# Post-norm decoder layer on one core: bias scaling to ScalarE, context passes to POOL, first key packings shared between two queues, two v transposes moved

## The reference, cut to what matters

```python
x = layernorm(x + attention(x))          # 32 heads of 32, qkv = x @ qkvw + qkvb, softmax, then @ ow + ob
q1 = fake_quant(x, x1_scale, x1_zp)      # (clip(round(x/s + z), 0, 255) - z) * s
q2 = fake_quant(ctx, x2_scale, x2_zp)    # ctx: 2 batches of 1024 x 1024
x = layernorm(x + matmul(q1, q2))
x = layernorm(x + lora_moe_ffn(x))       # base matmul, 8 experts of rank 16, top 2
```

## Time and profile before

| | |
|---|---|
| median of 3 runs | 778.38 us (775.95 to 780.17) |
| the profiled execution | 779.7 us, its span 777.9 us |
| mean granted TensorE clock | 0.970 |
| TensorE busy | 733.4 us, 94% of the span |
| VectorE, ScalarE, POOL busy | 482.5, 428.4 and 200.7 us |
| steps 0 and 1 / steps 2 to 17 / what follows | 5 to 52 us / to about 500 us / to 778 us |

### The profile page before, as it was taken

The page is one execution under the profiler, slowest core; times in us unless marked ns, Lnnn a source line. Parts: engine busy times, 40 slices in busy tenths (PEclk is TensorE's granted clock), DMA queues, the critical chain, the costliest instruction groups (busy, mean ns, idle before and its releaser), DMA issues.

```text
span 777.9 us, 11948 instructions
## 1 busy us (share of the span) xinstructions
PE 733.4 (94%) x3567; PEld 538.4 (69%) x3576; DVE 482.5 (62%) x853; ACT 428.4 (55%) x924; POOL 200.7 (26%) x149
## 2 busy tenths in 40 slices
PE   7889999999999999999999997889999977999996
PEld 5668668668767767767766842367767756788884
DVE  6767566557556656656755753456676778566554
ACT  5348668668668668667767785443434471212111
POOL 6260140240230230330330000033533374122111
PEclk9989999999999999999999986799999999999999
DMA  8735436436445445444442664274454121122101
GB/s 296 232 93 186 111 84 193 110 87 191 111 98 177 111 110 163 115 131 138 115 116 76 217 185 135 80 234 161 140 185 142 74 83 55 59 78 93 70 28 54
DMA packets 55553, 99.45 MB, mean 128 GB/s; under 512 B 11104, under 2 KB 22112, under 8 KB 54624
## 3 DMA queue, kind: packets, MB, share of 16 engines
q1 hardware_dynamic: 54944, 98.26, 41.4%
q10 hardware_dynamic: 576, 0.79, 0.4%
HBM read 56.54 MB, written 16.91 MB: 94 GB/s over the span
## 4 chain that ended last, share of the span: by engine, by line
PE 61%; issue 16%; DVE 10%; POOL 5%; DMA 3%; SPq 2%; ACT 2%; ACTq 1%; DVEq 0%; POOLq 0%
PE bank L459 35%; PE bank L522 8%; PE bank L548 8%; PE bank L562 6%; POOL xb L1093 2%; DVE st L1307 2%; POOL mv L1043 1%; DMA ctx_scratch<-ctxs 1%; PE bank L478 1%; ACTq L828 1%; DMA xres<-in_x 1%; DVE x1s L1405 1%; PE bank L675 1%; POOL xres L1038 1%; DVE big_lo L1342 1%
## 5 line engine op out<-in xcount | busy, mean ns | idle before, releaser
L801 ACT ACTIVATE probs<-bank 128x512 f32<-128x512 f32 x256 | 154.8, 606 | 128.8 <-PE bank L548 126.2
L1231 DVE TENSOR_REDUCE m_col<-bank 128x1 f32<-128x512 f32 x256 | 172.3, 687 | 80.1 <-PE bank L522 79.5
L806 ACT ACTIVATE bank<-bank,m_col 128x512 f32<-128x512 f32 x256 | 171.4, 670 | 19.1 <-DVE m_col L1231 13.4
L459 PE MATMUL bank<-big_hi,w_hi 128*128 128x512 f32 x384 | 157.7, 411 | 5.4 <-DVE big_lo L1123 5.4
L459 PE MATMUL bank<-big_lo,w_hi 128*128 128x512 f32 x384 | 153.5, 400 | 0.0
L459 PE MATMUL bank<-big_hi,w_lo 128*128 128x512 f32 x384 | 151.9, 396 | 0.0
L522 PE MATMUL bank<-kp,qp 96*128 96x512 f32 x256 | 106.5, 416 | 4.4 <-ACT bank L806 4.4
L548 PE MATMUL bank<-qp,kp 98*128 98x512 f32 x256 | 109.7, 430 | 0.0
L459 PEld LDWEIGHTS bank<-big_hi,w_hi 128*128 128x128 f32 x384 | 73.8, 192 | 24.3 <-DVE big_lo L1123 5.9
L1028 POOL TENSOR_SCALAR c_raw<-c_raw,sc 128x1024 f32<-128x1024 f32 x16 | 19.3, 1203 | 270.7 <-DMA c_raw<-in_ctx 265.1
L459 PEld LDWEIGHTS bank<-big_hi,w_lo 128*128 128x128 f32 x384 | 73.4, 191 | 17.2
(11 more groups left out here) (137 smaller groups left out, 1045.6 us busy)
## 6 DMA issues: line engine op xcount, KB each, us to landing
w_raw<-in_wqkv SPq DMA_DIRECT2D x7, 1536.0 KB, 8.8
c_raw<-in_ctx SPq DMA_DIRECT2D x16, 512.0 KB, 4.0
qp<-q_hi SPq DMA_DIRECT2D x128, 64.0 KB, 2.0
kp<-k_hi SPq DMA_DIRECT2D x120, 64.0 KB, 2.0
big_raw<-in_xT SPq DMA_DIRECT2D x16, 256.0 KB, 5.7
qp<-q_lo SPq DMA_DIRECT2D x64, 64.0 KB, 2.0
c_scratch<-c_q SPq DMA_DIRECT2D x16, 256.0 KB, 2.2
r_all<-r_scratch SPq DMA_DIRECT2D x64, 64.0 KB, 2.0
```

The source lines that it names most:

```text
L459: mm = nc.tensor.matmul(dst, lhs[a], rhs[b], start=(k == 0 and n == 0) if first is None else False, stop=(k == last_k and n == 2))
L801: nc.scalar.activation(probs[:, j, t, :], bank(ST0 + i % 2), ACT.Exp).then_inc(sem["exp_ok"], 1)
L806: nc.scalar.activation(bank(MAX[n % 3]), bank(MAX[n % 3]), ACT.Exp, bias=m_col[:, n:n + 1], accum_out=l_col[:, 1 - par, n:n + 1]).then_inc ...
L1231: nc.vector.reduce_max(m_col[:, n:n + 1], bank(MAX[n % 3]), AX, negate=True).then_inc(sem["rowmax"], 1)
```

## The change

ScalarE scales the q bias, before it rounds the v weights; DVE no longer does. POOL does all three passes over a context tile, one behind the other. For the keys of unit 0 ScalarE issues only heads 0 and 1; SyncE issues those of heads 2 and 3 between its q packings, and its load of the next weights in step 0 stands behind all packings. The v transpose of step 1 stands at slot 8 (was 16), that of step 2 at slot 8 (was at the start), both into PROJ0, and DVE's copies of both stand after maximum n = 2.

```diff
@@ SyncE, step
                     if begin:
                         pack(s, par, 1, "q")
-                    else:
-                        wait_alone(sp, sem["lo_ok"], 2 * s + 2)
+                    wait_alone(sp, sem["lo_ok"], 2 * s + 2)
+                    if not begin:
                         pack(s, par, 0, "k")
                         pack(s, par, 1, "k")
-                    if begin:
-                        load_w()
                     if 2 not in early:
                         pack(s, par, 2, "q")
...
                 if proj:
-                    if not begin:
-                        pack(s, par, 2, "k")
+                    pack(s, par, 2, "k")
                     if 3 not in early:
                         pack(s, par, 3, "q")
-                    if not begin:
-                        pack(s, par, 3, "k")
+                    pack(s, par, 3, "k")
+                    if begin:
+                        load_w()
@@ TensorE
-                        mm = nc.tensor.transpose(bank(ST0 + 1 if second else PROJ0, t * P, (t + 1) * P), vT[:, t * P:(t + 1) * P], ident[:, :])
+                        mm = nc.tensor.transpose(bank(PROJ0, t * P, (t + 1) * P), vT[:, t * P:(t + 1) * P], ident[:, :])
...
-                        if piece == 1 and second:
-                            pe.wait_ge(sem["lo_ok"], 2)
-                        elif piece == 1:
+                        if piece == 1:
                             pe.wait_ge(sem["v_ok"], s)
...
-                            pe.wait_ge(sem["v_ok"], 1)
...
-                if maxima and not second:
+                early = isinstance(s, int) and 1 <= s <= 2
+                if maxima and not early:
                     transpose_v()
...
-                    if second and q == 2 * KT:
+                    if early and q == KT:
                         transpose_v()
@@ ScalarE
             split_x(0, range(KT))
+            act.wait_ge(sem["bias_in"], 16)
+            nc.scalar.activation(bias[:, :, 0], bias[:, :, 0], ACT.Copy, scale=SM_SCALE).then_inc(sem["scale_q"], 1)
             act.wait_ge(wv_in, 16)
...
-                if not prev:
-                    pack_first_keys(2)
-                    pack_first_keys(3)
@@ POOL, step
                     if isinstance(s, int) and s == 0:
-                        pool.wait_ge(sem["sc_ok"], 3)
+                        pool.wait_ge(sem["sc_ok"], 4)
                     nc.gpsimd.tensor_scalar(c_raw[:, :], c_raw[:, :], sc[:, 6:7], sc[:, 3:4], ALU.mult, ALU.add).then_inc(sem["ctxq_1"], 1)
+                    wait_alone(pool, sem["ctxq_1"], s + 1)
+                    nc.gpsimd.tensor_scalar(c_raw[:, :], c_raw[:, :], 0.0, QMAX, ALU.max, ALU.min).then_inc(sem["ctxq_2"], 1)
+                    wait_alone(pool, sem["ctxq_2"], s + 1)
+                    if not isinstance(s, int) or s >= 1:
+                        wait_alone(pool, sem["c2_out"], 16 * s)
+                    nc.gpsimd.tensor_scalar(c_q[:, :], c_raw[:, :], MAGIC, consts[:, 2:3], ALU.add, ALU.subtract).then_inc(sem["ctxq_ok"], 1)
@@ VectorE
-            dve.wait_ge(sem["bias_in"], 16)
-            nc.vector.tensor_scalar(bias[:, :, 0], bias[:, :, 0], SM_SCALE, None, ALU.mult).then_inc(sem["scale_q"], 1)
             dve.wait_ge(sem["scale_q"], 1)
...
-                if maxima and not second:
+                early = isinstance(s, int) and 1 <= s <= 2
+                if maxima and not early:
                     copy_v()
...
-                    if second and n == 4:
+                    if early and n == 2:
                         copy_v()
...
-                    if proj and n == 8 and not begin:
-                        clip_context(s)
...
-                    if second and n == 2:
-                        clip_context(0)
-                    if second and n == 3:
-                        round_context(0)
-                    if proj and n == 13 and not begin:
-                        round_context(s)
```

More of the change, by code:

```diff
@@ L1197, in low @@
                                                    hi[:, :].bitcast(f32), ALU.add, ALU.subtract).then_inc(sem["lo_ok"], 1)
[L1199 to L1203, removed]
-                    nc.vector.tensor_scalar(c_raw[:, :], c_raw[:, :], 0.0, QMAX, ALU.max, ALU.min).then_inc(sem["ctxq_2"], 1)
-                def round_context(s):
-                    dve.wait_ge(sem["ctxq_2"], s + 1)
-                    nc.vector.tensor_scalar(c_q[:, :], c_raw[:, :], MAGIC, consts[:, 2:3], ALU.add, ALU.subtract).then_inc(sem["ctxq_ok"], 1)
                 second = isinstance(s, int) and s == 1
@@ L1217, in copy_v @@
                         dve.wait_ge(sem["pv_mm"], s - 2)
-                    nc.vector.tensor_copy(v_nat[:, 1 - par].rearrange("p t c -> p (t c)"), bank(ST0 + 1 if second else PROJ0)).then_inc(sem["v_ok"], 1)
-                if maxima and not second:
+                    nc.vector.tensor_copy(v_nat[:, 1 - par].rearrange("p t c -> p (t c)"), bank(PROJ0)).then_inc(sem["v_ok"], 1)
+                early = isinstance(s, int) and 1 <= s <= 2
+                if maxima and not early:
                     copy_v()
```

## The result

The changed kernel takes 784.62 us in the median of five runs (783.46 to 785.89), the kernel before 778.45 us beside it: the ratio is 1.0076, 95% interval 1.0053 to 1.010. It is 6.2 us slower, where 3.7 us faster was forecast; the interval lies clear of 1. The profiled execution took 783.85 us for a span of 782.0.

The account below looks back on a forecast made before the run. TensorE, busy 94% of the span, was taken as the bound. Gains of 2.9 (step 2's opening), 0.5 (clock) and 0.3 (later steps) sum to 3.7 us: 774.7 us against the 778.4 median, range 771.2 to 778.5.

Parts of the forecast that it names:

- What bounds the kernel: Whole kernel: TensorE, busy 94% of the span; from step 2 on its own matmuls set the 28.60 us period.
- The gaps removed: TensorE in step 1: the 2.75 us gap at 30 us and the 2.00 us before 50.40 go.
- the new last wait: Opening of step 2: TensorE waits for POOL's q weights, ready at 49.4 us instead of 52.28; gain 2.9 us.
- The price of the forms: POOL's three passes over a context tile: priced from nearest rows at 3.85 us, bounds 3.3 and 6.0.
- The landing: Tile 1 loaded behind the moved weight load on SyncE: taken as 9.0 us, landing at 40.5 (bounds 39.7 and 44.7).
- The base: Opening of step 2 at 52.28 us in the one earlier profile, against which the 2.9 us gain was counted.
- The clock: TensorE's clock before step 2: falls in a 2.8 us gap and costs 2.5 us against 3.0 before; 0.5 us gained.
- Steps 2 to 15: Later attention steps: VectorE's clip no longer held up by POOL in odd steps; 0.3 us gained.
- rival 2: Tile 1 not held by the weights, landing by 37 to 38 us: gain 6.7 us, 771.7 us; chance 0.09.
- Rival 3: Moved weight load makes POOL late, tile 1 landing after 43.4 us: 2.2 us lost, 780.6 us; chance 0.08.
- Rival 1: TensorE's clock does not fall before step 2: gain 6.2 us, 772.2 us; chance 0.27.
- Rival 4: ScalarE held by something else, or v's copy replaces the gap; step 1 shifts little: gain about 0.5, 777.9 us; chance 0.10.

## Why the prediction was wrong

**What bounds the kernel** was right: from step 2 on the period is TensorE's 28.60 us, and taking VectorE's passes away was worth 0.26 us over thirteen steps.

**The gaps removed** were right. Score 3 no longer waits, the maxima end by 45.6 us, and vT would have let step 2 open at 47.9. So was **the new last wait**: POOL's w_lo releases the first projection of step 2. But it was forecast for 49.4 us and came at 56.8. Of these 7.4 us, 5.2 are the passes over tile 1 and 2.4 POOL's later start on the tile (42.95 for 40.5), less 0.2 of smaller terms. A gain of 2.9 us against the 52.28 of before became a loss of 4.6, of which the clock gave 0.75 back: 3.8 of the 3.9 us at the product. Three things were wrong, in the order of their weight.

1. The price of the forms, the step that failed. "The nearest rows for the others are the same operation (1.21) and the one on constants (1.06)". These rows were all mult/add, down to the copy into w_hi, which the kernel before writes on POOL as times 1.0 plus 0.0 (1.05 us); max/min and add/subtract take 3.64 and 3.72. Three passes were put at 3.85 us and take 9.04 with their gaps; the upper bound of 6.0 rested on the 2.40 us of a two-input operation and was too low too. Replacing the forms alone gives 4.7 us back. Tile 0 was late as well: "tile 0's passes end at 31.3, before SyncE asks" came out as 36.8, and SyncE issued the load of tile 1 five microseconds behind the weight load instead of one. That cost next to nothing here, since tile 1 landed 10.9 us after the weight load's issue, and 10.6 where it was issued 1.1 us behind the weights. With the weight load early, tile 0 takes its place as what holds tile 1 (POOL started on it at 42.17). So two limits lay close together, and removing one alone brought little.
2. The landing. Scaling the 7.3 us of step 4 to 8.2 and taking 9.0 was too low: 10.6 and 10.9 us from the weight load's issue to the tile's landing, in the cheap forms and with the passes back on VectorE, where the tile stood right behind. The row in which the tile went first and landed in 3.8 is no guide for a tile that goes last. The 256 KB store behind the weights took 7.4 us instead of 2.2, which agrees with the ring-order rule of the Trainium skill (DMA: Bandwidth & Descriptors, Queues, rings and completion order). That the queue is the cause isn't shown, though. The same view as the earlier trace rows has this row of the other queue, ScalarE's, for a transfer that took 3.1 us when issued just before the weight load; no run issued the tile on another queue.

```profile
kp<-k_lo ACTq DMA_DIRECT2D x1, 64.0 KB, 8.2
```

3. The base. The gain of step 2's opening was counted from the one profile of before, with its rounding at 2.98 us and its clock down: the slowest of three executions at that place. The mean of the three products is 78.1; the changed kernel's 84.08 stands 6.0 us behind that mean, near the 6.2 us of the medians. Three profiles don't prove a mean, and a product doesn't tell a total, so this part of the account is likely and not shown. What is shown is that the forecast counted as a gain a loss of clock and of rounding that two of the three executions did not have in full.

The clock was forecast to fall and to cost 2.5 us, and did fall; 4.5 us of work at half speed are 2.25 us lost. But it fell in a gap of 9.78 us, not in one of 2.8. Steps 2 to 15 gained 0.26 us (371.90 for thirteen steps against 372.16), as forecast; the second profile of before has 372.01, so two executions of the one kernel differ by 0.15 here. Two slips in the arithmetic changed nothing: the three passes and their gaps add up to 3.88 and not 3.85, and the range starts at 771.2 where rival 2 gives 771.7.

**The rivals.** Rival 3 had the direction and the place: POOL late with the weights, step 2 opening at 56.8 where its worst case was 54.8. Its cause was not the main one. It blamed the moved weight load and a tile landing after 43.4 us; the tile landed at 42.75, and POOL's passes alone, with the load at its old place, bring most of the loss. It had been given 0.08 because the passes were priced from rows of another kind. Rival 1 (the clock stays up) and rival 2 (tile 1 by 37 to 38 us) did not come; rival 2's 3.8 us landing was the furthest from what was seen. Rival 4 missed as well: without ScalarE's six issues the wait before score 3 is gone.

## What to carry to other kernels

A row prices only its own operation codes: before work is moved to POOL, find a row with the same pair of operations, and if there is none, let the upper bound be several times the cheapest. When an engine that gates another takes on more work, look at the order in its queue first; here putting the gating split ahead of the new passes gave 6.9 us, cheap forms for the passes 4.7. And take a second profile of the kernel before, if a gap of the first is to be counted as a gain.

## What the runs showed of the hardware that was not expected

On POOL, tensor_scalar over 128x1024 elements took 1.05 us as mult/add (1.20 with per-partition operands), 2.78 us with any of the five single operations tried, and 3.6 to 3.7 us with any other pair tried, mult/max included. Mult/add, max/min and add/subtract took the same in steps 0 and 1 and behind the context work. Two cheap passes (1.04 and 1.12 us) replaced one add/subtract pass of 3.72 with the same result.

Transfers issued right behind 1536 KB on the same queue landed after it: 256 KB in 7.4 us instead of 2.2, 512 KB in 9.5 instead of 3.4. A 64 KB packing on the other queue took 8.2 us at such a time, instead of 3.1 just before the 1536 KB were issued, so a second queue alone is not shown to help.

VectorE's rounding (0.74 us) that met a two-input operation on POOL ended 0.55 us after it, at 1.83 and 2.98 us; in a third execution the rounding was not held, and POOL's operation took 2.96 us instead of 2.39.

What stays open is how often VectorE's rounding meets POOL's w_lo in the kernel before, and where the rest of the spread of its runs (774.7 to 782.6 us over all comparisons) comes from. Part of it lies behind the attention: in the two profiles of before, the time from the product of step 15 to the end is 325.6 and 327.1 us.
